# Converting the second weight matrix inside the last pair of the first stage

## The chip, the cores and the metric

The program runs on one core of a Trainium2 chip. Its time is the device time of one execution in microseconds, us. The kernel before took 2138.25 us, the median of three runs (2136.12 to 2142.62 us). The execution that the profiler recorded took 2138.95 us, and its span, first to last instruction, is 2137.1 us.

## The reference

The input x has 10000 rows of 1024 columns, and there are 5000 edges (src, dst). Two layers follow each other:

```python
# layer 1: a graph convolution on the normalised rows
h = einsum('nd,od->no', layernorm(x), W) + b
deg = (edges that start in a row) + 1
norm = deg[row]**-0.5 * deg[col]**-0.5     # row, col: src, dst and the self loops
x = x + segment_sum(norm[:, None] * h[col], row)
# layer 2: a feed-forward layer with low-rank experts
z = layernorm(x)
base_out   = einsum('bsi,oi->bso', z, base_W) + base_b
shared_out = (z @ shared_A.T) @ shared_B.T
gate = softmax(z @ router_W.T + router_b);  the two largest are kept, normalised
routed_out = sum over 6 experts of gate * ((z @ routed_A.T) @ routed_B.T)
x = x + base_out + shared_out + routed_out
```

All is float32. The kernel splits each operand of a product into a high part (the value rounded by a copy to the type fp32r) and a low part (value minus high part), and adds three products: high by high, high by low, low by high.

## The kernel before

The 10000 rows are padded to 79 tiles of 128 rows. There are two stages, and the second reads rows that the first has written to DRAM.

**First stage.** It computes the rows h and the rows r = x plus the self term, and stores both (`h_rows`, `r_rows`). Seven tiles go singly, then 36 pairs of tiles, each by seven block products in place of eight (a Strassen scheme). The products are called A11, S1, S2, A12, S3, A22, S4 in the order in which TensorE (PE) runs them; each has 12 matmuls of 512 columns. A11 of a pair is run ahead, within the pair before. The weights have seven quarters, B11, T1, T2, B21, T3, T4, B22, one for each product in that order, and lie in seven regions of the on-chip memory. `product_at(p, n)` is the count of the semaphore `done` at which product n of pair p is finished. The names A11 to S4 and B11 to B22 are the numbers 0 to 6, so B11 stands for the product A11, T1 for S1, T2 for S2, B21 for A12, T3 for S3.

For each pair the results are four half rows: C11 and C21 are written by ScalarE (ACT) in `weigh_part`, C22 and C12 by VectorE (DVE) in `finish_part`. `weigh_sum` on ACT copies a running sum out of a bank of the accumulator memory (PSUM) into u2 or u3. PE's product A22 waits for u3 (`u3_ok`), and S4 waits for C22 (`part_ok[C22]`). Each finished half row is stored by SyncE's queue (SP) in `store_part`. After all four, DVE computes two rows r (`residual`, L1406) and SP stores them.

**Between the stages.** The second weights are 8 blocks of 128 by 1142 values (`load_base`, L480), with 113 rows of small weights beside them (`bl_raw`). Each block is split by `base_high(k)` on ACT (L918) and `base_low(k)` on DVE (L1541), and the small weights likewise (L999, L1548). These blocks overwrite the regions of the first weights: block 0 to 2 as loaded lie in the region of B11, blocks 3 to 6 reach into that of T1, block 7 into T2, and the high parts lie in T2, B21 and, for blocks 6 and 7, T3. Hence the waits on `done`.

GpSimd (POOL) waits until the four half rows of the last pair have landed in DRAM (L694), passes a branch (L695) that is not taken when no row has too many edges, signals `rows_ready`, and then begins the gathers: it runs a one-column instruction that carries a wait (`carry_wait`, L552) and issues the indirect DMAs (L746, L728) which fetch rows of `h_rows` by edge. SP loads `r_rows` (L538) after `rows_ready` and after all rows r are stored.

**Second stage.** A software pipeline over 79 tiles: gathered rows are added to r on DVE, normalised on DVE, POOL and ACT, transposed and split, and multiplied with the 8 blocks on PE (L1032 to L1034, 72 matmuls a tile). Each engine goes through its instructions in the order in which they are written; there is no planner. The order is what the change touches.

Of the kernel before, what the change touches and what calls it, by code (L numbers as in the profile page):

```python
# [5 lines left out]
F32 = mybir.dt.float32  # L6
# [4 lines left out]
ALU = mybir.AluOpType  # L11
# [11 lines left out]
KB = D // P  # L23
# [29 lines left out]
PAIRS = (TILES - HEAD) // 2  # L53
A11, S1, S2, A12, S3, A22, S4 = range(7)
B11, T1, T2, B21, T3, T4, B22 = range(7)
# [81 lines left out]
def gnn_ffn(nc, x, src, dst, w_t, b, base_t, b_low, router_b, out, deg_dram, spill_dram):  # L137
# [4 lines left out]
    with ExitStack() as ctx:  # L142
# [140 lines left out]
        base_lo, o = place("base_lo", [P, KB, BCOLS], F32R)  # L283
        base_raw = sb("base_raw", [P, KB, BCOLS], F32, o)
        base_hi = sb("base_hi", [P, KB, BCOLS], F32R)
# [109 lines left out]
        def product_at(p, n):  # L395

            if n == A11:
                return max(7 * p - 1, 1)
            return 7 * p + 1 + n + (n > S3 and p + 1 < PAIRS)
# [11 lines left out]
        def _(sp):  # L411
# [56 lines left out]
            def store_part(p, v):  # L468
                t, h = PARTS[v]
                sp.wait_ge(part_ok[v], p + 1)  # L470
                sp.dma_start(h_dram[rows(first(p) + t), half(h)], hrow[t][:, half(h)]) \
                    .then_inc(part_stored[v], 16)
# [13 lines left out]
            for p in range(PAIRS):  # L486
                if p == 0:
                    store_rows(HEAD - 1)
                else:
                    store_part(p - 1, C12)  # L490
                    for t in range(2):
                        store_rest(p - 1, t)
                if p == PAIRS - 1:
                    for n, ks in ((B11, range(3)), (T1, range(3, 7)), (T2, range(7, KB))):
                        sp.wait_ge(done, product_at(p, n))
                        for k in ks:
                            load_base(k)
                store_part(p, C11)
                if p > 0 and first(p - 1) + 6 < TILES:
                    sp.wait_ge(r_stored, 16 * first(p))  # L500
                    load_x(first(p - 1) + 6)
                    load_x(first(p - 1) + 7)
                if RANK_AT <= p + 1 < RANK_AT + CHUNKS // RANKED and p >= RANK_AT:
                    sp.wait_ge(ranked, p + 1 - RANK_AT)
                    load_sources(p + 1 - RANK_AT)
                if p == RANK_AT - 1:
                    sp.wait_ge(t_lo_ok, 16)
                    load_sources(0)
                if p == TABLE_AT:
                    sp.wait_ge(slots_put, 16 * CHUNKS)  # L510
                    sp.dma_start(offs[:].rearrange("p t r -> p (t r)"),
                                 slot_dram[0:SLOTS, :].rearrange("(p s) a -> p (s a)", p=P)) \
                        .then_inc(slots_in, 16)
                store_part(p, C22)
                if p == PAIRS - 1:
                    sp.wait_ge(done, product_at(p, T3))
                    for a, z in ((0, KLOW - 1), (KLOW - 1, KLOW)):
                        sp.dma_start(bl_raw[a:z, :], b_low[a:z, :]).then_inc(bl_in, 16)
                store_part(p, C21)
# [235 lines left out]
        def _(act):  # L755
# [144 lines left out]
            def weigh_part(p, v, n):  # L900

                t, h = PARTS[v]
                act.wait_ge(done, product_at(p, n))
                if p == 0:
                    act.wait_ge(dis_ok, len(FACTORS))
                    act.wait_ge(r_ok, HEAD - 1 + (t == 0))
                    act.wait_ge(h_stored[t], 16 * ((HEAD - 1 - t) // 2 + 1))
                else:
                    act.wait_ge(part_stored[v], 16 * p)
                    act.wait_ge(pair_r_ok, 2 * (p - 1) + t + 1)  # L910
                nc.scalar.activation(hrow[t][:, half(h)], bp[p % 2][BANK[n]][:], ACT.Copy,
                                     scale=dis[:, first(p) + t:first(p) + t + 1]) \
                    .then_inc(part_ok[v], 1)

            def base_high(k):
                act.wait_ge(weights_in[k], 48)
                act.wait_ge(done, product_at(PAIRS - 1, T3))
                nc.scalar.activation(base_hi[:, k, :], base_raw[:, k, :], ACT.Copy) \  # L918
                    .then_inc(rest_hi_ok, 1)

# [48 lines left out]
            for p in range(PAIRS):  # L969
                last_high(p)  # L970
                weigh_sum(p, S2, 0, u2, C12, u2_ok)
                if p + 1 < PAIRS:
                    first_row(p + 1)
                weigh_part(p, C11, A12)
                if p + 1 < PAIRS:
                    first_row_right(p + 1)
                    normalise(first(p + 1) + 1)
                    if p > 0:
                        begin_third(p + 1)
                weigh_sum(p, S3, 1, u3, C22, u3_ok)  # L980
                if p + 2 < PAIRS:
                    begin_first(p + 2)
                if p + 1 < PAIRS:
                    begin_second(p + 1)
                    second_row(p + 1)
                    sums_high(p + 1)
                if p + 2 < PAIRS:
                    normalise(first(p + 2))
                if p == PAIRS - 1:
                    base_high(0)  # L990
                    base_high(1)
                weigh_part(p, C21, A22)
                if p + 1 < PAIRS:
                    others_high(p + 1)

            for k in range(2, KB):
                base_high(k)
            act.wait_ge(bl_in, 32)
            nc.scalar.activation(bl_hi[:], bl_raw[:], ACT.Copy).then_inc(rest_hi_ok, 1)  # L999
# [233 lines left out]
        def _(dve):  # L1233
# [167 lines left out]
            def residual(p, t, vs):  # L1401

                for v in vs:
# [2 lines left out]
                nc.vector.scalar_tensor_tensor(xn[n % 6][:], xn[n % 6][:], sqd[:, n:n + 1],  # L1406
                                               hrow[t][:], ALU.mult, ALU.add).then_inc(pair_r_ok, 1)

            def left_low(p, n, raw):
                dve.wait_ge(left_hi_ok, left_at(p, n))  # L1410
                nc.vector.tensor_tensor(left_lo[n][:].rearrange("p k n -> p (k n)"), raw,
                                        left_hi[n][:].bitcast(F32).rearrange("p k n -> p (k n)"),
                                        ALU.subtract).then_inc(left_lo_ok, 1)
# [84 lines left out]
            for p in range(PAIRS):  # L1498
                if p == 0:
                    finish_rows(HEAD - 1)  # L1500
                    quarter_low(T4, t4, 12)
                else:
                    finish_part(p - 1, C12, S4, u2, u2_ok)
                left_low(p, S4, s4[:])
                if p == SLOT_AT + 2:
                    dve.wait_ge(max_done, 1)
                    link(nc.vector.tensor_reduce(over_max[0:1, :], bt[0][0:1, 0:P], AX.X, ALU.max))
                    nc.vector.tensor_copy(spill_flag[:], over_max[0:1, :]).then_inc(tables_ok, 1)
                if p > 0:
                    residual(p - 1, 0, (C11, C12))  # L1510
                    residual(p - 1, 1, (C22, C21))
                if p + 1 < PAIRS:
                    statistics(first(p + 1) + 1)
                    left_low(p + 1, A11, a11[:])
                    scales(first(p + 1) + 1)
                if RANK_AT <= p < RANK_AT + CHUNKS // RANKED:
                    ranks(p - RANK_AT)
                if p == SLOT_AT:
                    slot_table()
                if p == TABLE_AT + 1:  # L1520
                    dve.wait_ge(slots_in, 16)
                    link(nc.vector.tensor_scalar(taken[:], offs[:, :, 0:SKIPPED], float(NPAD), None,
                                                 ALU.is_lt))
                finish_part(p, C22, S1, u3, u3_ok)
                if p + 1 < PAIRS:
                    sums(p + 1)
                    if p + 2 < PAIRS:
                        statistics(first(p + 2))
                    left_low(p + 1, A12, left_raw[A12][:])
                    if p + 2 < PAIRS:  # L1530
                        scales(first(p + 2))
                    left_low(p + 1, A22, bt[1][:])
                    dve.wait_ge(s3_ok, p + 2)
                    left_low(p + 1, S3, left_raw[S3][:])
# [1 line left out]
            residual(PAIRS - 1, 0, (C11, C12))  # L1536
            residual(PAIRS - 1, 1, (C22, C21))

            def base_low(k):
                dve.wait_ge(rest_hi_ok, k + 1)  # L1540
                nc.vector.tensor_tensor(base_lo[:, k, :], base_raw[:, k, :],  # L1541
                                        base_hi[:, k, :].bitcast(F32), ALU.subtract) \
                    .then_inc(rest_lo_ok, 1)

            for k in range(KB):
                base_low(k)
            dve.wait_ge(rest_hi_ok, KB + 1)
            nc.vector.tensor_tensor(bl_lo[:], bl_raw[:], bl_hi[:].bitcast(F32), ALU.subtract) \  # L1548
# [198 lines left out]
```

## Time and profile before

| what | value |
|---|---|
| median of three runs | 2138.25 us |
| the profiled execution | 2138.95 us, its span 2137.1 us |
| PE busy | 2049.0 us (96%) |
| DVE busy | 1601.0 us (75%) |
| POOL busy | 793.7 us (37%) |
| ACT busy | 703.7 us (33%) |
| mean clock granted to PE | 0.986 of full |
| DMA, mean over the span | 155 GB/s |

The page cuts the span into 40 slices of 53.4 us. Each engine's line gives its busy share in tenths for each slice, 9 meaning 90% or more. The line PEclk gives the clock granted to PE in tenths of full. A wait is listed as the instruction that was idle, the arrow, and what it was released by. Times "from the span's start" are used throughout.

### The profile page before, as it was taken

How to read it: one execution, taken by the hardware profiler on the slowest of the kernel's cores; microseconds unless marked ns; L12 is line 12 of the kernel's file. 1: busy time of each engine (PE TensorE's matmuls, PEld its weight loads, DVE VectorE, ACT ScalarE, POOL GpSimd, SP SyncE). 2: the span in 40 equal slices, each digit the busy share in tenths (PEclk: the TensorE clock that was granted, in tenths of full speed). 3: DMA queues.
4: the chain of work that ended last, by engine and by line, in shares of the span. 5: the costliest groups of instructions: out<-in, count | busy, mean ns of one | idle time of the engine just before them, and what ended most of it. 6: DMA issues, size and time to landing. Idle time of an engine off the chain costs nothing.

```text
span 2137.1 us, 34748 instructions
## 1 busy us (share of the span) xinstructions
PE 2049.0 (96%) x11145; PEld 1880.3 (88%) x11145; DVE 1601.0 (75%) x4089; ACT 703.7 (33%) x1236; POOL 793.7 (37%) x932
## 2 busy tenths in 40 slices
PE   7999999999999999739999999999999999999999
PEld 6777777777787777539999999999999999999999
DVE  6877878787776666657777777777777777777774
ACT  4455555555555555411111112111111112121111
POOL 1802333333325200164344444444444444444430
PEclk9999999999999999969999999999999999999999
DMA  6523434343434534566555656555555656555541
GB/s 249 199 104 144 165 134 174 132 173 134 169 125 153 146 134 162 215 170 167 147 164 146 166 158 162 156 153 159 150 164 149 166 152 162 153 156 159 151 128 40
DMA packets 126946, 330.63 MB, mean 155 GB/s; under 512 B 32944, under 2 KB 35840, under 8 KB 126806
## 3 DMA queue, kind: packets, MB, share of 16 engines
q1 hardware_dynamic: 77462, 226.31, 30.1%
q0 software_dynamic: 49344, 102.80, 21.0%
q8 instruction: 46, 0.75, 0.2%
q14 instruction: 94, 0.77, 0.1%
HBM read 266.46 MB, written 125.55 MB: 183 GB/s over the span
## 4 chain that ended last, share of the span: by engine, by line
PE 53%; issue 26%; DVE 9%; POOL 8%; ACT 2%; DMA 1%; DVEq 0%; POOLq 0%; ACTq 0%
PE bo L1032 13%; PE bo L1033 13%; PE bo L1034 13%; PE bt L1064 3%; POOL counted L638 2%; POOL counts L652 2%; PE bo L1223 2%; POOL xpw L580 2%; PE bo L1227 2%; PE bo L1225 2%; POOL slots L659 2%; DVE xn L1406 1%; PE bo L1042 1%; PE bo L1046 1%; PE bo L1044 1%
## 5 line engine op out<-in xcount | busy, mean ns | idle before, releaser
L1032 PE MATMUL bo<-base_hi,z_hi 128*128 128x380 f32 (+1 forms) x1896 | 652.7, 344 | 9.1 <-issue 9.1
L1033 PE MATMUL bo<-base_lo,z_hi 128*128 128x380 f32 (+1 forms) x1896 | 639.0, 337 | 0.0
L1034 PE MATMUL bo<-base_hi,z_lo 128*128 128x380 f32 (+1 forms) x1896 | 638.9, 337 | 0.0
L1053 PE MATMUL bo<-wr_hi,left_hi 128*128 128x512 f32 x1008 | 402.7, 399 | 6.3 <-ACT bo L880 3.8
L1057 PE MATMUL bo<-wr_hi,left_lo 128*128 128x512 f32 x1008 | 394.2, 391 | 0.0
L1055 PE MATMUL bo<-wr_lo,left_hi 128*128 128x512 f32 x1008 | 393.9, 391 | 0.0
L1032 PEld LDWEIGHTS bo<-base_hi,z_hi 128*128 128x128 f32 x1896 | 357.8, 189 | 9.5 <-issue 9.5
L1034 PEld LDWEIGHTS bo<-base_hi,z_lo 128*128 128x128 f32 x1896 | 358.7, 189 | 0.0
L1033 PEld LDWEIGHTS bo<-base_lo,z_hi 128*128 128x128 f32 x1896 | 358.5, 189 | 0.0
L746 POOL DMA_INDIRECT g<-h_rows,row_now x237 | 306.6, 1294 | 90.3 <-issue 90.1
L580 POOL TENSOR_TENSOR xpw<-xpin,neg_half 128x1 f32<-128x1 f32 x79 | 72.5, 918 | 551.8 <-DVE xpin L1248 551.8
L1053 PEld LDWEIGHTS bo<-wr_hi,left_hi 128*128 128x128 f32 x1008 | 189.9, 188 | 56.8 <-issue 20.4
L1004 ACT ACTIVATE ex<-lg 128x6 f32<-128x6 f32 x79 | 16.4, 208 | 659.5 <-DVE lg L1650 659.5
L1057 PEld LDWEIGHTS bo<-wr_hi,left_lo 128*128 128x128 f32 x1008 | 189.7, 188 | 40.3
L1055 PEld LDWEIGHTS bo<-wr_lo,left_hi 128*128 128x128 f32 x1008 | 190.1, 189 | 36.3
L735 POOL TENSOR_TENSOR pw<-pin,neg_half 128x1 f32<-128x1 f32 x79 | 47.1, 596 | 460.5 <-DVE pin L1617 460.5
L1604 DVE SCALAR_TENSOR_TENSOR acc<-g,taken,acc 128x1024 f32<-128x1024 f32 x158 | 202.9, 1284 | 19.9 <-DMA g<-h_rows,row_now 9.0
L1639 DVE SCALAR_TENSOR_TENSOR acc<-acc,dis,bo 128x262 f32<-128x262 f32 (+2 forms) x237 | 126.1, 569 | 108.1 <-PE bo L1227 103.0
L1020 ACT ACTIVATE z<-acc,shift,scale 128x1024 f32<-128x1024 f32 x79 | 98.4, 1245 | 287.2 <-DVE shift L1629 287.2
L764 ACT ACTIVATE un<-xn,xshift,xscale 128x1024 f32<-128x1024 f32 x79 | 98.3, 1244 | 262.9 <-issue 262.5
L728 POOL DMA_INDIRECT g<-h_rows,row_now x79 | 124.5, 1576 | 39.1 <-issue 39.1
L1244 DVE BATCH_NORM_STATS2 xst<-xn 128x6 f32<-128x512 f32 x158 | 109.1, 690 | 10.1 <-DMA xn<-x 7.3
(176 smaller groups left out, 2975.9 us busy)
## 6 DMA issues: line engine op xcount, KB each, us to landing
xn<-x SPq DMA_DIRECT2D x79, 512.0 KB, 4.3
r_rows<-xn SPq DMA_DIRECT2D x79, 512.0 KB, 2.7
acc<-r_rows SPq DMA_DIRECT2D x79, 512.0 KB, 4.3
out<-acc SPq DMA_DIRECT2D x79, 512.0 KB, 4.8
h_rows<-hrow SPq DMA_DIRECT2D x144, 256.0 KB, 2.5
g<-h_rows,row_now POOLq DMA_INDIRECT x316, 6.2
base_raw<-base_t SPq DMA_DIRECT2D x8, 571.0 KB, 8.4
wr_raw<-w_t SPq DMA_DIRECT2D x16, 256.0 KB, 6.7
```

Source lines behind the costliest of these rows:

```text
L580: nc.gpsimd.tensor_tensor(xpw[t % 2][:], xpin[t % 2][:], neg_half[:, 0:1], ALU.pow) \
L728: nc.gpsimd.indirect_dma_start(g[q][SKIPPED][:], None, h_dram, bass.IndirectOffsetOnAxis(ap=row_now[q][:, ROUNDS - 1:ROUNDS], axis=0), bou ...
L746: nc.gpsimd.indirect_dma_start(g[q][r][:], None, h_dram, bass.IndirectOffsetOnAxis(ap=row_now[q][:, r:r + 1], axis=0), bounds_check=(NPAD ...
L1032: nc.tensor.matmul(ps, hi[:, k, :], m_hi[:, k, n], start=(k == 0), stop=False)
L1033: nc.tensor.matmul(ps, hi[:, k, :], m_lo[:, k, n], start=False, stop=False)
L1034: return nc.tensor.matmul(ps, lo[:, k, :], m_hi[:, k, n], start=False, stop=(ends and k == KB - 1))
L1053: nc.tensor.matmul(ps, left_hi[n][:, k, :], wr_hi[n][:, k, :], start=False, stop=False, skip_group_check=True)
L1055: nc.tensor.matmul(ps, left_hi[n][:, k, :], wr_lo[n][:, k, :], start=False, stop=False, skip_group_check=True)
L1057: last = nc.tensor.matmul(ps, left_lo[n][:, k, :], wr_hi[n][:, k, :], start=False, stop=(k == 3), skip_group_check=True)
L1244: rows_c.link(dve, nc.vector.bn_stats(xst[q][:, h, :], xt[:, half(h)]))
L1604: accs.link(dve, nc.vector.scalar_tensor_tensor(a[:], g[q][r][:], taken[:, bass.ds(n, 1), r], a[:], ALU.mult, ALU.add))
L1639: nc.vector.scalar_tensor_tensor(av, av, dis[:, bass.ds(t, 1)], ps, ALU.mult, ALU.add).then_inc(out_ok, 1)
```

## The change

Three loads go out one pair earlier, and six of the eight conversions are moved into the last pair's time. SP loads blocks 0 to 2 within the last pair but one, after its half row C22, once the last pair's A11 is finished. ACT converts blocks 0 to 2 between C11 and u3 of the last pair, and blocks 3 to 5 after u3, where blocks 0 and 1 stood. The wait in front of blocks 0 to 5 is for A12 of the last pair, in place of S3. DVE takes the low parts of blocks 0 to 2 ahead of C22 and those of 3 to 5 ahead of C12. The rest stays behind the last pair. No conversion, load or product is added or dropped.

```diff
@@ SP, in the loop over pairs
                 if p == PAIRS - 1:
-                    for n, ks in ((B11, range(3)), (T1, range(3, 7)), (T2, range(7, KB))):
+                    for n, ks in ((T1, range(3, 7)), (T2, range(7, KB))):
                         sp.wait_ge(done, product_at(p, n))
                         for k in ks:
                             load_base(k)
...
                 store_part(p, C22)
+                if p == PAIRS - 2:
+                    sp.wait_ge(done, product_at(PAIRS - 1, B11))
+                    for k in range(3):
+                        load_base(k)
@@ ACT
             def base_high(k):
                 act.wait_ge(weights_in[k], 48)
-                act.wait_ge(done, product_at(PAIRS - 1, T3))
+                act.wait_ge(done, product_at(PAIRS - 1, B21 if k < 6 else T3))
...
                 weigh_part(p, C11, A12)
+                if p == PAIRS - 1:
+                    for k in range(3):
+                        base_high(k)
...
                 if p == PAIRS - 1:
-                    base_high(0)
-                    base_high(1)
+                    for k in range(3, 6):
+                        base_high(k)
                 weigh_part(p, C21, A22)
...
-            for k in range(2, KB):
+            for k in range(6, KB):
                 base_high(k)
@@ DVE
+                if p == PAIRS - 1:
+                    for k in range(3):
+                        base_low(k)
                 finish_part(p, C22, S1, u3, u3_ok)
+                if p == PAIRS - 1:
+                    for k in range(3, 6):
+                        base_low(k)
...
-            for k in range(KB):
+            for k in range(6, KB):
                 base_low(k)
```

The function `base_low` itself only moves up in the text.

## Rows read from the trace of the kernel before

**Rows 1.** The page's slices: PE's busy share in tenths.
```profile
PE   7999999999999999739999999999999999999999
```
**Rows 2.** Windows: start:end and length, then busy us of PE, PEld, DVE, ACT, POOL, clock, DMA.
```profile
1605.00:2100.00 495.00, 494.25 (x2970) 491.98 (x2969) 378.68 (x1086) 92.00 (x198) 210.04 (x250) 1.00 0.55 149
```
**Rows 3.** The chain of waits between the stages: start, us, what held it.
```profile
895.39 0.76 DVE hrow L1397
896.17 6.93 DMA h_rows<-hrow
...
904.11 0.52 issue
...
910.15 1.11 POOL g L746
```
**Rows 4.** Timeline of POOL: start, us, instruction, [idle before, releaser].
```profile
903.55 6.43 POOL L552 TENSOR_TENSOR tick_pool<-neg_half 128x1 f32<-128x1 f32 x1 [34.52 <-DMA h_rows<-hrow]
955.72 1.08 POOL L552 TENSOR_TENSOR tick_pool<-neg_half 128x1 f32<-128x1 f32 x1 [0.76 <-DMA g<-h_rows,row_now]
```
**Rows 5.** Line L552 on POOL: count, duration in ns min/median/max.
```profile
L552 POOL TENSOR_TENSOR tick_pool<-neg_half x199: 182/193/6433, 172.2 to 2063.7; 128x1 f32<-128x1 f32 x199
```
**Rows 6.** Timeline of DVE, end of the first stage and one later place.
```profile
898.65 10.15 DVE L1541 TENSOR_TENSOR base_lo<-base_raw,base_hi 128x1142 fp32r<-128x1142 f32 x8
908.71 1.22 DVE L1548 TENSOR_TENSOR bl_lo<-bl_raw,bl_hi 113x1024 fp32r<-113x1024 f32 x1
916.37 2.60 DVE L1604 SCALAR_TENSOR_TENSOR acc<-g,taken,acc 128x1024 f32<-128x1024 f32 x2 [6.44 <-DMA g<-h_rows,row_now]
955.53 1.22 DVE L1612 TENSOR_TENSOR acc<-acc,g 128x1024 f32<-128x1024 f32 x1
```
**Rows 7.** Timeline of ACT in the last pair.
```profile
886.12 0.69 ACT L911 ACTIVATE hrow<-bo,dis 128x512 f32<-128x512 f32 x1 [2.03 <-PE bo L1057]
888.83 0.69 ACT L897 ACTIVATE u<-bo,dis 128x512 f32<-128x512 f32 x1 [2.03 <-PE bo L1057]
889.42 2.19 ACT L918 ACTIVATE base_hi<-base_raw 128x1142 fp32r<-128x1142 f32 x2
899.87 1.16 ACT L918 ACTIVATE base_hi<-base_raw 128x1142 fp32r<-128x1142 f32 x1 [0.67 <-DMA base_raw<-base_t]
```
**Rows 8.** Timeline of PE: an earlier gap, last A22, start of second stage, later gap.
```profile
732.26 1.06 PE L1064 MATMUL bt<-ident,un 128*128 128x128 f32 x8 [3.15 <-DVE left_lo L1411]
889.67 0.47 PE L1053 MATMUL bo<-wr_hi,left_hi 128*128 128x512 f32 x1 [0.87 <-ACT u L897]
928.18 1.97 PE L1064 MATMUL bt<-ident,z 128*128 128x128 f32 x8 [32.83 <-ACT z L1020]
954.90 0.34 PE L1217 MATMUL bt<-ident,hs 128*113 128x128 f32 x1 [2.65 <-DVE z_lo L1683]
```
**Rows 9.** Timeline of SP's queue: a half-row store of pair 34, the base loads.
```profile
872.60 0.33 SPq L471 DMA_DIRECT2D h_rows<-hrow  x1
882.56 5.24 SPq L480 DMA_DIRECT2D base_raw<-base_t  x8
```
**Rows 10.** Line L471 (half-row stores), from 840 to 910 us.
```profile
DMA to landing us min/median/max: 2.0/2.5/12.3
```
**Rows 11.** Line L480 (base loads).
```profile
DMA to landing us min/median/max: 5.6/8.4/12.8
```
**Rows 12.** Line L538 (loads of r_rows), from 860 to 930 us.
```profile
DMA to landing us min/median/max: 3.3/7.5/13.8
```
**Rows 13.** Windows of 2 us, columns as in rows 2.
```profile
874.00:876.00 2.00, 2.00 (x11) 1.65 (x10) 1.97 (x4) 1.91 (x5) 0.00 (x0) 1.00 0.06 23
898.00:900.00 2.00, 0.00 (x0) 0.00 (x0) 2.00 (x3) 1.28 (x2) 0.00 (x0) 0.50 1.06 375
904.00:906.00 2.00, 0.00 (x0) 0.00 (x0) 2.00 (x2) 0.00 (x0) 2.00 (x1) 0.50 0.04 16
956.00:958.00 2.00, 2.00 (x8) 1.80 (x6) 1.93 (x3) 1.05 (x2) 1.84 (x2) 0.50 0.08 23
```

More of the change, by code:

```diff
@@ L1407, in residual, with base_low @@
                                                hrow[t][:], ALU.mult, ALU.add).then_inc(pair_r_ok, 1)
+            def base_low(k):
+                dve.wait_ge(rest_hi_ok, k + 1)
+                nc.vector.tensor_tensor(base_lo[:, k, :], base_raw[:, k, :],
+                                        base_hi[:, k, :].bitcast(F32), ALU.subtract) \
+                    .then_inc(rest_lo_ok, 1)
             def left_low(p, n, raw):
@@ L1537, in _ @@
             residual(PAIRS - 1, 1, (C22, C21))
[L1539 to L1543, printed above, removed]
-            for k in range(KB):
+            for k in range(6, KB):
                 base_low(k)
```

## The prediction

> **What bounds the kernel now.** I read the page's slices first. PE is full in all but three slices of 53.4 us: the first, and the two from 855 to 962 us, where it falls to 7 and 3 tenths [rows 1]. PE's own rows give the reason: one wait of 32.83 us, until 928.18, for the first normalised tile of the second stage [rows 8]. After that start PE is busy 494.25 of 495 us [rows 2], so the second stage lasts as long as its matmuls, wherever it begins. A microsecond gained or lost ahead of that start is a microsecond of the end. The change touches nothing outside this place, and the question is what the 32.8 us consist of.
>
> The chain of waits gives it in order [rows 3]. DVE, which waits for the last product, writes the last half row C12 from 895.39 on (0.76 us); its store lands after 6.93 us; POOL starts its waiting instruction L552 at 903.55; and the first gather goes out at 910.15. The reader is to see that the piece between the two is the interesting one: L552 is recorded with 6.43 us [rows 4], while its median over 199 is 193 ns [rows 5]. It ended at 909.98. DVE's eight low parts and the small one run without a break from 898.65 to 909.93 [rows 6]. The same coincidence stands elsewhere: the L552 of 955.72 lasts 1.08 us and ends at 956.80, and DVE's L1612 ends at 956.75 [rows 4, 6]. I read this as POOL being held while DVE runs operations on two operands of the on-chip memory. If so, the conversions are on the path, through POOL and not through PE, which needs the blocks only some 30 us later.
>
> **The change part by part, against the profiled execution (2138.95 us).**
>
> Loads. Blocks 0 to 2 go out behind the store of pair 34's C22 at 872.60, so from about 873 us; three issues at 5.24/8 = 0.66 us each end near 875, before that pair's next store is due (its ACT result comes at about 876). The DMA engines are nearly free there (share 0.06 at 874 to 876 [rows 13]). SP waits for A11 of the last pair, which is through by then, so nothing queues behind this wait. Cost nothing. In the last pair five loads stand where eight stood, from 882.56 on [rows 9]. At 375 GB/s [rows 13] a block of 0.585 MB takes 1.56 us, so 4.7 us of transfer leave the saturated time.
>
> Store of C12. It was issued at about 896.2 and took 6.93 us [rows 3], where half-row stores have a median of 2.5 us [rows 10]. The extra 4.4 us I read as the backlog of base loads, the last of which lands only at 899.87 [rows 7]. With 4.7 us less traffic the backlog is gone before C12. Bounds: 2.0 us (shortest row) to 6.93 us (unchanged). I take 3, near the median because that row is of the same transfer with free engines.
>
> ACT ahead of u3. C11 starts at 886.12 and the next ACT instruction can start 0.59 us later, as block 0 does after u3 (888.83 to 889.42 [rows 7]). Three conversions at a pitch of 1.04 (2.19 for two, less the last one's 1.15) to 1.16 (one alone) take 3.1 to 3.5 us, so u3 starts at 889.8 to 890.2 instead of 888.83. PE's A22 starts 0.84 us after u3 [rows 7, 8]: at 890.7 to 891.0 instead of 889.67. Nothing hides this; PE ends its last product 1.0 to 1.4 us later, and I take 1.2. This is the price of the change.
>
> ACT and DVE after it. Blocks 3 to 5 occupy ACT from 890.6 to 894.0; A22 ends at about 893.6 (from 889.67 to C12 at 895.39 PE ran two products, 24 matmuls, 2.75 us a product at 0.23 each with 0.2 until DVE starts), so C21 is late by 0.3 us, and it isn't the last half row. Block 5 must have landed by 892.8: it is the third of its batch, first landing 5.6 us after 882.56 [rows 11] plus two blocks, 891.3 us. On DVE the low parts run at a pitch of 1.26 us ((908.71 - 898.65)/8 [rows 6]). Blocks 0 to 2 end at about 891.7, when block 2 comes from ACT at 890.05; C22 (0.76 like C12) follows until 892.5, and S4 isn't due on PE before 893.6. Cover 1.1 us. Blocks 3 to 5 end at about 896.2, and S4 ends at 896.4. Cover only 0.2 us; if block 5 is later than thought, C12 and all behind it slip by the same amount.
>
> DVE at the end. Before, from the start of C12 (895.39) to the end of the small low part (909.93) it was 14.54 us without a pause. Six low parts leave: 6 x 1.26 = 7.55, and 6.99 remain. C12 starts at 896.6, so DVE is done at 903.6. C12 lands at 897.4 + 3 = 900.4, and POOL arrives at 900.8, within DVE's run, as before. It is freed at 903.6 instead of 909.98, and the first gather goes out at 903.85 instead of 910.15: 6.3 us earlier.
>
> From there everything shifts with it, with one new meeting. The loads of r_rows start once the last rows r are stored. They were issued behind DVE's residuals, which shift by 1.2 us only, so the load of the first r tile (1.4 us of transfer) meets the first gathers, where there was a free stretch before (share 0.04 at 904 to 906 [rows 13]). Bounds 0 to 1.4 us; I take 0.2, since the gathers' data follow their issue by some 2 us.
>
> Sum: +1.2 (u3) - 7.55 (six low parts) + 0.05 (rounding) + 0.2 = -6.1 us. The profiled execution would take 2132.85 us. It lies 0.7 us above the median of the runs shown, so by the median 2138.25 - 6.1 = 2132.2 us.
>
> A rule of the Trainium skill speaks to the held instruction. "SBUF — State Buffer", in the part on engine and DMA ports, says that a VectorE operation with two SBUF inputs and a GpSimd instruction that reads SBUF exclude each other for one whole instruction, the loser blocking. The rows show the exclusion, but over more than one instruction: the L552 of 903.55 let four ends of DVE instructions go by and came through only at the end of the run. If the lock were given up at each instruction, POOL would have passed near 904.8 already. I go by the rows; the other reading is the first rival.
>
> **The rivals.**
>
> POOL gets in early. If the hold is released at the first end of a DVE instruction, or if DVE has a pause in front of block 6, POOL passes right at 900.8 and the gather goes out at 901.5 (0.19 for L552, 0.52 issue [rows 3, 5]). Gain 8.6 us, 2129.6 us. Against it are the ends passed over at 905 to 908.7. Chance 0.12.
>
> The store is not shortened. C12 lands after 6.93 us again, at 904.3, and DVE is done by then. The gather goes out at 904.8 + 0.71 = 905.5. Gain 4.6 us, 2133.6 us. For it speaks that the small loads and the store of C21 still stand ahead of it; against it, the median of 2.5. Chance 0.10.
>
> DVE isn't what holds POOL. If the 6.6 us between POOL's arrival and the first gather are a fixed cost of this start (a branch stands in front of it), only the store's backlog is won: 900.8 + 6.6 = 907.4, gain 2.8 us, 2135.5 us. Against it are the two ends that agree within 0.05 us. Chance 0.10.
>
> The clock falls in the gap ahead of A22. The gap grows from 0.87 to about 2.1 us. A gap of 3.15 us at 729 to 732 left the clock at full; one of 2.65 us before 954.90 was followed by half clock from 956 on [rows 8, 13]. If it falls, the 24 matmuls of A22 and S4 cost up to 24 x 0.23 = 5.4 us more, nearly the whole gain: about 2137.6 us. Chance 0.06.
>
> Slower than before: the load of the first r tile queues behind the gathers. DVE's first instruction of the second stage needs it and the first gathered rows; before, it started at 916.37 on the gathers' landing [rows 6]. Loads of this line take from 3.3 to 13.8 us [rows 12]. By the forecast DVE starts there 6.1 us earlier, at 910.3. A load issued at about 903.2 has 7.1 us until then, and each further microsecond goes off the gain; from 13.2 us on the gain is gone, and at 13.8 us it lands at 917.0, 0.6 us later than before: 2138.9 us. For it: the load and the gathers start together now. Against it: the load's issue is still ahead of the gathers'. Chance 0.04.
>
> **How the numbers follow.** Forecast 0.58, rivals 0.12, 0.10, 0.10, 0.06, 0.04. About 0.3% (6.4 us) is what a measurement can tell from no change; faster means below 2131.8 us. The forecast lies almost on this line: half of it counts as faster (0.29), with the first rival 0.41. Slower by 0.3% needs two mishaps: 0.03. The range takes the forecast's own 2130.5 to 2134, the first two rivals and the third: 2129 to 2136.5 us.
>
> **What would show it.** L552 between the stages should take some 3 us and end with DVE's small low part, near 903.6. The store of C12 should take about 3 us, the gap ahead of A22 about 2 us at full clock, and the three early loads should stand at 873 us. DVE's run behind C12 should hold two low parts. The first gather should stand near 904, PE's long wait should be 25.5 us (32.8, begun 1.2 later, ended 6.1 earlier). The prediction is wrong if L552 keeps its 6.4 us with DVE idle, if u3 or C12 start later than 890.3 or 897.2, or if the time from first gather to first transposes (18.0 us) changes by more than 1 us.

## The result, and the profile after

The changed kernel takes 2130.24 us, the median of 6 runs (2126.13 to 2132.16), against 2137.8 us for the kernel before on the same chip (6 runs). The ratio is 0.9967, 95% interval 0.9956 to 0.9977. Timed once more on another chip, with 7 runs, it gave 2131.22 against 2136.89 us, ratio 0.9970 (0.9959 to 0.9982). The forecast was 2132.2 us, 6.1 us below the kernel before; measured were 7.6 and 5.7 us. The profiled execution has a span of 2130.3 us (before: 2137.1).

The three early loads stand where the prediction put them, as SP's timeline of the changed kernel shows; this answers to [rows 9]:

```profile
873.64 1.40 SPq L480 DMA_DIRECT2D base_raw<-base_t  x3
```

Then the chain of waits of the changed kernel between the stages, which answers to [rows 3]. L552 is L556 here, and L746 is L750.

```profile
898.70 0.76 DVE hrow L1404
...
899.48 2.02 DMA h_rows<-hrow
...
901.94 0.56 POOL tick_pool L556
...
903.51 2.03 POOL g L750
```

The store of C12 takes 2.02 us instead of 6.93, POOL's waiting instruction is followed by the first gather at 903.51 instead of 910.15, but C12 itself begins 3.3 us later than in [rows 3] (0.7 us of it because the whole last pair stands later in this execution). POOL's own timeline of the changed kernel, which answers to [rows 4]:

```profile
901.94 1.41 POOL L556 TENSOR_TENSOR tick_pool<-neg_half 128x1 f32<-128x1 f32 x1 [32.24 <-DMA h_rows<-hrow]
903.51 2.03 POOL L750 DMA_INDIRECT g<-h_rows,row_now  x1 [0.16 <-issue]
```

And DVE's, which answers to [rows 6]:

```profile
888.56 3.87 DVE L1418 TENSOR_TENSOR base_lo<-base_raw,base_hi 128x1142 fp32r<-128x1142 f32 x3 [5.74 <-ACT base_hi L922]
...
893.01 3.85 DVE L1418 TENSOR_TENSOR base_lo<-base_raw,base_hi 128x1142 fp32r<-128x1142 f32 x3
898.70 0.75 DVE L1404 SCALAR_TENSOR_TENSOR hrow<-bo,dis,u 128x512 f32<-128x512 f32 x1 [1.84 <-PE bo L1064]
...
901.95 2.60 DVE L1418 TENSOR_TENSOR base_lo<-base_raw,base_hi 128x1142 fp32r<-128x1142 f32 x2
904.47 1.22 DVE L1561 TENSOR_TENSOR bl_lo<-bl_raw,bl_hi 113x1024 fp32r<-113x1024 f32 x1
912.58 2.60 DVE L1617 SCALAR_TENSOR_TENSOR acc<-g,taken,acc 128x1024 f32<-128x1024 f32 x2 [6.89 <-DMA g<-h_rows,row_now]
```

The low parts of blocks 0 to 5 stand ahead of C12, and the run behind it is two low parts and the small one. From the start of C12 to the end of the run it is 905.69 - 898.70 = 6.99 us, as forecast. But POOL's L556 (901.94, 1.41 us) ended at 903.35, with the end of the first of these low parts, 2.3 us ahead of the run's end. ACT's timeline of the changed kernel in the last pair answers to [rows 7]:

```profile
886.79 0.69 ACT L915 ACTIVATE hrow<-bo,dis 128x512 f32<-128x512 f32 x1 [2.03 <-PE bo L1064]
887.38 3.23 ACT L922 ACTIVATE base_hi<-base_raw 128x1142 fp32r<-128x1142 f32 x3
890.52 0.68 ACT L901 ACTIVATE u<-bo,dis 128x512 f32<-128x512 f32 x1
891.09 3.24 ACT L922 ACTIVATE base_hi<-base_raw 128x1142 fp32r<-128x1142 f32 x3
```

PE's rows for the last A22 and for the start of the second stage answer to [rows 8]:

```profile
891.34 0.47 PE L1060 MATMUL bo<-wr_hi,left_hi 128*128 128x512 f32 x1 [1.86 <-ACT u L901]
...
922.31 1.97 PE L1071 MATMUL bt<-ident,z 128*128 128x128 f32 x8 [23.65 <-ACT z L1027]
```

Then the changed kernel's windows around that gap, columns as in [rows 2]; the last three numbers are the granted clock, the DMA share and GB/s:

```profile
890.00:892.00 2.00, 0.66 (x3) 0.61 (x4) 2.00 (x2) 2.00 (x3) 0.00 (x0) 1.00 1.01 388
892.00:894.00 2.00, 2.00 (x7) 1.54 (x6) 2.00 (x3) 2.00 (x3) 0.00 (x0) 0.59 0.94 360
894.00:896.00 2.00, 2.00 (x7) 1.57 (x6) 2.00 (x3) 0.39 (x2) 0.00 (x0) 0.56 0.91 281
896.00:898.00 2.00, 2.00 (x10) 1.66 (x9) 0.86 (x1) 2.00 (x3) 0.00 (x0) 1.00 0.48 189
```

The gap ahead of A22 is 1.86 us, and behind it the clock is down to half (1.2 GHz) for most of the time from 892.3 to 895.7: matmuls stand 0.43 us apart instead of 0.23.

Executions of one kernel differ by some microseconds in how long the first stage takes (the last pair's u2 starts between 881.9 and 887.9 us in the profiles below, and at 883.39 and 884.96 in the two of the kernel before). So I measure all places from the start of u2; of what the edits move, only the three early loads stand ahead of it:

| kernel | u3 | C12 | POOL arrives | first gather | first transposes | first products |
|---|---|---|---|---|---|---|
| before | 5.44 | 12.00 | 20.16 | 26.76 | 44.79 | 55.89 |
| before, again | 5.44 | 12.00 | 20.85 | 26.75 | 44.46 | 55.57 |
| changed | 6.45 | 14.63 | 17.87 | 19.44 | 38.24 | 49.06 |
| changed, again | 6.45 | 14.61 | 17.85 | 19.42 | 38.94 | 50.15 |
| changed, third | 6.45 | 14.64 | 17.87 | 19.45 | 38.35 | 49.11 |
| loads only (e1) | 5.44 | 12.00 | 15.25 | 16.82 | 38.44 | 49.43 |
| conversions only (e7) | 8.63 | 17.66 | 21.62 | 22.47 | 42.04 | 53.24 |
| before, low parts late (e2) | 5.44 | 12.00 | 19.62 | 20.38 | 44.39 | 52.70 |
| the same, second profile (e8) | 5.44 | 12.00 | 20.86 | 21.62 | 45.41 | 53.65 |
| conversions in idle (e3) | 5.44 | 12.00 | 15.41 | 16.81 | 36.32 | 47.18 |
| the same, tail late (e4) | 5.44 | 12.00 | 16.83 | 17.59 | 37.79 | 49.62 |
| e3 with the first low part early (e11) | 5.44 | 12.00 | 16.35 | 17.11 | 36.24 | 39.67 |
| loads only, POOL later (e9) | 5.44 | 12.00 | 19.26 | 26.75 | 44.79 | 56.27 |
| loads only, POOL later, with a memset (e10) | 5.44 | 12.00 | 19.29 | 26.75 | 44.69 | 56.10 |

"POOL arrives" is the start of its first waiting instruction, L552 (or L556). Each entry is a start read from the kernel's timelines, less the start of u2 there (before: 883.39; changed: 884.07). After the first products PE runs to the end in 1194.3 to 1197.8 us in all but e11.

### The profile page after: what moved, and what is told of

It reads as the page before. It is cut to its first block, busy times and chain, and to the rows that moved or that the text cites. A ratio compares the mean times of both kernels' runs of the same rounds, so it can differ in the third digit from the quotient of the medians.

```text
span 2130.3 us, 34748 instructions
## 1 busy us (share of the span) xinstructions
PE 2051.9 (96%) x11145; PEld 1883.3 (88%) x11145; DVE 1600.5 (75%) x4089; ACT 703.4 (33%) x1236; POOL 788.0 (37%) x932
## 4 chain that ended last, share of the span: by engine, by line
PE 55%; issue 25%; POOL 8%; DVE 8%; ACT 2%; DMA 1%; DVEq 0%; POOLq 0%; ACTq 0%
PE bo L1039 14%; PE bo L1040 14%; PE bo L1041 14%; PE bt L1071 4%; POOL counted L642 2%; POOL counts L656 2%; PE bo L1230 2%; PE bo L1234 2%; POOL xpw L584 2%; PE bo L1232 2%; POOL slots L663 2%; PE bo L1049 1%; PE bo L1051 1%; PE bo L1053 1%; DVE xn L1413 1%
## 5 line engine op out<-in xcount | busy, mean ns | idle before, releaser
L750 POOL DMA_INDIRECT g<-h_rows,row_now x237 | 308.3, 1301 | 90.7 <-issue 90.7
```

What stands on the lines that cost most here:

```text
L750: nc.gpsimd.indirect_dma_start(g[q][r][:], None, h_dram, bass.IndirectOffsetOnAxis(ap=row_now[q][:, r:r + 1], axis=0), bounds_check=(NPAD ...
```

## The experiments

The theories: A, POOL is held until DVE's whole run of low parts ends, as forecast; B, POOL passes at the next end of a DVE instruction; C, the time between POOL's arrival and the first gather is fixed. And beside them the question which half of the change carries the gain.

**The loads alone (e1).**
```diff
@@ the kernel before, SP
-                    for n, ks in ((B11, range(3)), (T1, range(3, 7)), (T2, range(7, KB))):
+                    for n, ks in ((T1, range(3, 7)), (T2, range(7, KB))):
...
+                if p == PAIRS - 2:
+                    sp.wait_ge(done, product_at(PAIRS - 1, B11))
+                    for k in range(3):
+                        load_base(k)
```


> The kernel before with the change's loads alone: blocks 0 to 2 behind the last but one pair's C22, all conversions where they were. Both theories: the store of C12, issued at about 896.2, lands in 2 to 3 us instead of 6.93, and POOL arrives at L552 at about 899.2 instead of 903.55. Theory A (POOL is held until DVE's run of low parts ends): L552 then lasts 10.7 us, the first gather stays at 910.15, the time is the one of before (0.0 us). Theory B (POOL passes at the end of one DVE instruction): L552 ends at a boundary of the low parts, 900 to 901.3, the first gather goes out at about 901.5, and the time falls by 4 to 8 us. Theory C (a fixed 6.6 us from POOL's arrival to the first gather): gather at 905.8, time down by 4.3 us.

Measured: 2131.75 against 2137.81 us, ratio 0.9970 (0.9957 to 0.9983). The loads alone give as much as the whole change, within what the times can tell. Only the loads were moved, and the store of C12 took 2.02 us, so the backlog is confirmed as its cause. The timeline of POOL in this kernel:

```profile
903.14 1.40 POOL L556 TENSOR_TENSOR tick_pool<-neg_half 128x1 f32<-128x1 f32 x1 [29.61 <-DMA h_rows<-hrow]
904.71 2.03 POOL L750 DMA_INDIRECT g<-h_rows,row_now  x1 [0.16 <-issue]
907.04 2.12 POOL L750 DMA_INDIRECT g<-h_rows,row_now  x1 [0.30 <-issue]
909.46 2.19 POOL L750 DMA_INDIRECT g<-h_rows,row_now  x1 [0.30 <-issue]
911.68 0.41 POOL L556 TENSOR_TENSOR tick_pool<-neg_half 128x1 f32<-128x1 f32 x1
```

And of DVE:

```profile
903.14 10.15 DVE L1545 TENSOR_TENSOR base_lo<-base_raw,base_hi 128x1142 fp32r<-128x1142 f32 x8
...
914.35 2.60 DVE L1608 SCALAR_TENSOR_TENSOR acc<-g,taken,acc 128x1024 f32<-128x1024 f32 x2
```

POOL arrived as the run began and passed at the end of the first low part (1.40 us); then its gathers were issued 2.34 and 2.42 us apart, against 1.42 and 1.32 in the kernel before, where DVE was idle by then. Theory A fails here, and C as well. But DVE's first addition follows its run without a pause (914.35), and so the first transposes are 6.4 us earlier, not 9.9 like the first gather: with the gathers early, DVE's run is on the path by itself.

**The low parts held back until the first gather has landed, in the kernel before (e2, timed as e8).**
```diff
+            dve.wait_ge(g_in[0][SKIPPED], 16)
             for k in range(KB):
                 base_low(k)
```


> The kernel before, with DVE's eight low parts and the small one held back until the first gather has landed, so that DVE is idle when POOL arrives. Theories A and B: L552 takes its usual 0.19 us, and the first gather goes out at 904.3 instead of 910.15. Theory C (fixed cost): L552 still takes 6.4 us and the gather stays at 910.15. The whole time should not fall much, since the 11.3 us of low parts now start at about 908.6 and end at 920, later than the 916.37 at which DVE's first addition started: +3 us to the start of the second stage, more if POOL's next gathers are held by the run.

> The kernel before with DVE's low parts held back until the first gather has landed, timed. Its single execution took 2132.64 us, its first gather stood 20.4 us behind the start of u2 against 26.8 in the kernel before. If DVE's run in front of POOL's first gathers is what costs the kernel before: 3 to 6 us faster than before. If that execution was a draw: within 1.5 us of before.

Measured: e2 2132.64 us in one run, e8 2134.08 against 2138.14 us, ratio 0.9979 (0.9969 to 0.9988). With the store as slow as before (6.39 and 7.64 us) L552 took 0.19 us and the gather followed 0.76 us behind it, as POOL's timeline of e2 shows:

```profile
902.49 0.19 POOL L552 TENSOR_TENSOR tick_pool<-neg_half 128x1 f32<-128x1 f32 x1 [33.96 <-DMA h_rows<-hrow]
903.25 1.11 POOL L746 DMA_INDIRECT g<-h_rows,row_now  x1 [0.57 <-issue]
```

So DVE's run is what holds L552 in the kernel before; a fixed cost (C) is excluded. The first transposes came neither earlier nor the 3 us later that I had expected (44.39 and 45.41, against 44.79 and 44.46); of the gain of 4 us, 1.9 to 3.2 us stand at the next step, the first products, and where the rest comes from isn't shown. There DVE waited less for the second tile's gathers, which had landed meanwhile (in e2 its two waits were 0.82 and 1.85 us, in the kernel before 2.33 and 2.52). I had expected hardly any gain from e2 and was wrong on that; for e8 the 4.1 us lie in the range written for it.

**The kernel before and the changed one, profiled again (e5, e6, e12; no edit).**

> The kernel before, unchanged, profiled a second time. In the first profile POOL's L552 was held for 6.43 us, past four ends of DVE instructions, while in the loads-only kernel the same instruction met the same run of low parts and lasted 1.40 us. If POOL is always held to the end of DVE's run in this kernel: L552 lasts until the end of the small low part again, about 6.4 us. If what a POOL instruction waits for is normally one DVE instruction and the first profile was an unlucky draw: L552 lasts 0.2 to 2.6 us and the first three gathers are issued 2.3 to 2.5 us apart, ahead of the end of the run. The store of C12 takes 6 to 7 us in both.

> The changed kernel, unchanged, profiled a second time. The order of work says: gap ahead of A22 1.9 us, store of C12 about 2.0 us, L552 1.2 to 1.4 us, first gather at 19.4 us behind the start of u2 (in the first profile 884.07 to 903.51). The clock of the last pair may differ: if it falls after every gap of 1.9 us, A22 and S4 take 7.3 us again; if it is a draw, they take 5.7 us in some executions.

> The changed kernel, unchanged, timed beside the others on one chip. About 2130.5 us; the kernel with the conversions in ACT's idle stretches should stand 1.5 to 2.6 us below it. Its profile should show the gap of 1.86 us ahead of A22 with half clock behind it a third time, if such a gap always costs the clock at this place.

Measured for the kernel before (2139.54 us), first POOL's timeline:

```profile
905.81 5.73 POOL L552 TENSOR_TENSOR tick_pool<-neg_half 128x1 f32<-128x1 f32 x1 [35.22 <-DMA h_rows<-hrow]
```

Then DVE's last row of the run:

```profile
910.27 1.22 DVE L1548 TENSOR_TENSOR bl_lo<-bl_raw,bl_hi 113x1024 fp32r<-113x1024 f32 x1
```

L552 ended at 911.54 and the run at 911.49 (910.27 + 1.22). The long hold is no draw. The changed kernel repeats as well: L556 took 1.41, 1.41 and 1.42 us. The gap of 1.86 us was followed by half clock in all three profiles (C12 at 14.63, 14.61, 14.64), but that is no proof that it always is. PE has two gaps earlier in the first stage which no edit touches, and there one kernel goes either way. [rows 8] has 3.15 us of gap ahead of 732.26 in the kernel before, at full clock. In its second profile, e5, PE's timeline has this in the same place:

```profile
733.19 1.94 PE L1064 MATMUL bt<-ident,un 128*128 128x128 f32 x8 [3.42 <-DVE left_lo L1411]
```

And the window behind that gap:

```profile
733.00:735.00 2.00, 1.81 (x9) 1.84 (x10) 2.00 (x5) 0.96 (x3) 0.00 (x0) 0.50 0.23 83
```

The clock is at half (1.2 GHz), and eight transposes take 1.94 us in place of 1.06. Over all fourteen profiles the clock fell at this gap (2.20 to 3.94 us long) in five, and at another, near 643 us (2.25 to 2.29 us long), in seven. The two earlier gaps are a draw, then, and three of three ahead of A22 can't rule out a draw there. The 0.87 us of the other kernels was followed by full clock in ten profiles of ten.

The times were 2131.85 and, timed, 2131.22 us.

**POOL's arrival moved inside the run (e9, e10), in the loads-only kernel.**
```diff
                     pool.wait_ge(row_copied, t + 1)
+                    if isinstance(t, int) and t == 0:
+                        pool.wait_ge(rest_lo_ok, 3)
+                        nc.gpsimd.memset(tick_pool[:, 13:14], 0.0)     # e10 only
                     carry_wait(5 + 4 * (s.q % 2))
```


> The loads-only kernel, with POOL's L552 held back until DVE has ended the third of its eight low parts, so that it is issued within 0.1 us of an instruction's end, in the middle of the run and not at its start. If the long hold of the kernel before (6.43 and 5.73 us) comes from arriving in the middle of the run: L552 lasts 7 to 8 us, until the small low part ends. If POOL passes at the next end whenever it is in line at the start of a DVE instruction: 1.2 to 1.4 us.

> As the kernel in which POOL waits for the third low part's end, with a one-column memset (it only writes) ahead of L552, so that L552 arrives 0.2 to 0.6 us into the fourth low part. If the phase inside a DVE instruction decides: a long hold here (5 us or more) and a short one without the memset. If the place in the run decides: both alike. If neither: 0.7 to 1.1 us here, the rest of the fourth low part.

The timeline of POOL in e9:

```profile
901.55 7.33 POOL L556 TENSOR_TENSOR tick_pool<-neg_half 128x1 f32<-128x1 f32 x1 [33.64 <-DVE base_lo L1547]
```

Of DVE in e9:

```profile
897.54 10.15 DVE L1547 TENSOR_TENSOR base_lo<-base_raw,base_hi 128x1142 fp32r<-128x1142 f32 x8
907.61 1.22 DVE L1554 TENSOR_TENSOR bl_lo<-bl_raw,bl_hi 113x1024 fp32r<-113x1024 f32 x1
```

Of POOL in e10:

```profile
903.54 0.10 POOL L749 MEMSET tick_pool<- 128x1 f32 x1 [33.61 <-DVE base_lo L1548]
903.60 7.30 POOL L556 TENSOR_TENSOR tick_pool<-neg_half 128x1 f32<-128x1 f32 x1
```

Both were held to the run's end: 7.33 us, to 908.88, with the run's end at 908.83, and 7.30 us. The loads-only kernel with POOL arriving at the third low part's end has the first gather of the kernel before (26.75). So its late arrival alone takes away what the early loads had won; the times, 2135.28 and 2136.62 us, one run each, lie among those of the kernel before (2134.57 to 2138.79, median 2136.89). The stage's first L552 passed at the next end when it arrived before or within the run's first low part (e1, changed three times, e3, e7, e11), and was held to the end when it came later (before twice, e9, e10).

The phase within an instruction doesn't explain it. The two edits came out 0.03 us apart (0.23 and 0.26 us into the fourth low part), so the memset tests it hardly at all; but the kernel before arrived 1.13 us into a low part, e5 0.57 us, and both were held to the end too.

The place in the run is not the whole rule either. L552 runs again for the next gathers, and in the kernels with a long run some of these later ones fall in its middle. In e1 one begins at 911.68, in the seventh low part, and takes 0.41 us. In e2, first POOL's timeline:

```profile
913.10 1.20 POOL L552 TENSOR_TENSOR tick_pool<-neg_half 128x1 f32<-128x1 f32 x1
```

Then DVE's run in e2:

```profile
907.87 10.16 DVE L1541 TENSOR_TENSOR base_lo<-base_raw,base_hi 128x1142 fp32r<-128x1142 f32 x8 [9.66 <-DMA g<-h_rows,row_now]
```

At 1.26 us each, 913.10 lies in the fifth low part, which ends at 914.25. L552 ended at 914.30, with four instructions of the run still to come; e8 repeats it (1.20 us). These passed at the next end although they came in the middle of the run, 0.19 us into a low part. What sets them apart from the four that were held is that POOL had been at work since the run's first low part. A memset ahead of L552, which only writes, doesn't make the difference (0.10 us in e10, and L552 was held all the same). What does stays open.

**The conversions alone (e7).** The changed kernel with all eight loads where they were before: the edit is the reverse of e1's on SP.

> The changed kernel with all eight loads where they stood before: the conversions' new order alone. ACT stands at block 0 ahead of u3 until it lands, some 5.6 us after the first issue at 882.56, and at block 2 until about 891.4, so u3 starts near 892.5 instead of 888.8 and the gap ahead of A22 is 4.5 us, with the half clock after it. The backlog stays, less the 3.7 us by which C12 is late. If the early loads carry the gain (they shorten the store, and the conversions' order is only a cost): 1 to 4 us slower than before. If the six conversions taken out of DVE's run carry it: 2 to 4 us faster than before.

Measured: 2134.01 against 2138.14 us, ratio 0.9981 (0.9971 to 0.9990), 4.1 us faster, where 2 to 4 were expected. u3 is 3.2 us later (3.7 expected), PE's gap ahead of A22 is 4.05 us with half clock behind it, and C12 is 5.7 us later; yet the first gather is 4.3 us earlier. A late C12 meets no backlog (store 2.73 us), and POOL arrives in the run's first low part and passes after 0.69 us. So the conversions' order gains by the hold (0.69 us in place of 6.43), and pays for the store's gain with C12's lateness; the early loads gain by store and hold (2.02 and 1.40 us). The two halves overlap (4.1 and 6.1 us apart, 7.6 and 5.7 together), since both take POOL's first L552 out of the middle of DVE's run.

**The conversions where ACT is idle (e3).**
```diff
@@ the changed kernel, ACT
-                act.wait_ge(done, product_at(PAIRS - 1, B21 if k < 6 else T3))
+                act.wait_ge(done, product_at(PAIRS - 1, T2 if k < 2 else B21 if k < 6 else T3))
...
+                if p == PAIRS - 1:
+                    base_high(0)
+                    base_high(1)
                 weigh_part(p, C11, A12)
                 if p == PAIRS - 1:
-                    for k in range(3):
-                        base_high(k)
+                    base_high(2)
```


> The changed kernel with ACT's conversions of blocks 0 and 1 moved ahead of C11 (waiting for S2 of the last pair in place of A12), block 2 behind C11, and 3 to 5 behind u3 as they were, so that u3 is not delayed. If the delayed u3 and the half clock after it cost the changed kernel 1.0 and 1.6 us: the gap ahead of A22 is 0.9 us, no window in the last pair is below full clock, C12 starts 2.6 us earlier, and the time falls by 2 to 2.6 us against the changed kernel (about 2127.6). If these microseconds were hidden behind POOL's wait: no change within 1 us.

Measured: 2128.90 us (2128.05 to 2130.05) against 2137.81, ratio 0.9954 (0.9942 to 0.9967). ACT had 2.03 us idle ahead of C11 and 2.03 ahead of u3 [rows 7]; the three conversions fit there, as ACT's timeline of e3 shows:

```profile
886.17 2.20 ACT L922 ACTIVATE base_hi<-base_raw 128x1142 fp32r<-128x1142 f32 x2
888.31 0.69 ACT L915 ACTIVATE hrow<-bo,dis 128x512 f32<-128x512 f32 x1
888.89 1.15 ACT L922 ACTIVATE base_hi<-base_raw 128x1142 fp32r<-128x1142 f32 x1
891.03 0.69 ACT L901 ACTIVATE u<-bo,dis 128x512 f32<-128x512 f32 x1 [0.98 <-PE bo L1066]
```

And PE's row for the last A22:

```profile
891.86 0.47 PE L1062 MATMUL bo<-wr_hi,left_hi 128*128 128x512 f32 x1 [0.87 <-ACT u L901]
```

u3 is at 5.44 again, the gap at 0.87 us, the clock full, and C12 at 12.00: the 2.6 us are back. The first transposes come 1.9 to 2.6 us earlier than in the three profiles of the changed kernel. In time the ratios differ by 0.0013 and 0.0016, 2.8 to 3.4 us, with intervals that overlap, so the times alone don't show that it beats the changed kernel. They do show it for the loads alone, timed beside it on one chip (2130.66 to 2134.14 us, against 2128.05 to 2130.05).

**The same with DVE's tail behind the gather (e4).**
```diff
+            dve.wait_ge(g_in[0][SKIPPED], 16)
             for k in range(6, KB):
                 base_low(k)
```


> As the kernel with the conversions in ACT's idle stretches, and DVE's two last low parts and the small one held back until the first gather has landed. Theory A (POOL held to the end of DVE's run): the first gather goes out near 900.7 instead of about 903, and the second stage starts 0.5 us or more earlier, bounded by the 3.7 us of low parts that now sit between the first gathers' landing and the first addition. Theory B (POOL passes at the next end of an instruction): the gather moves by less than 1 us, and the second stage starts about 1.3 us later, since DVE is busy with low parts when the gathered rows land.

Measured: 2129.04 against 2137.81 us, ratio 0.9957 (0.9946 to 0.9969): the same as e3. L556 took 0.19 us, but its store took 3.61 us, so the first gather came 0.8 us later by the mark, not earlier, and the first transposes 1.5 us later, as theory B has it.

**e3 with the low parts of the second stage's first tile taken early (e11).**
```diff
-                if s.has(1):
+                if s.has(1) and s.has(0):
                     low_parts(s)
...
+                    if isinstance(s.i, int) and s.i == -2:
+                        low_parts(Step(-1, DEEP - 1))
                     acc_statistics(s)
```


> The kernel with the conversions in ACT's idle stretches, and in addition the low parts of the second stage's first tile taken on DVE ahead of the statistics of the second tile, where DVE waits some 2.4 us for a gather. PE's first products of the second stage then start near 927 instead of 932.8 and are over when the second tile is ready to be transposed. If PE's start is bound by its own order: 1.5 to 2.5 us faster than without this (about 2126.8). If the second tile's gathers bind it all the same: no change within 0.5 us.

Measured: 2127.54 against 2136.89 us, ratio 0.9959 (0.9945 to 0.9972). PE's first products start 7.5 us earlier by the mark, but PE then waits 4.14 us for z_lo of a later step, and all but 0.6 us is given back by the end (u2 to the end of the span 1242.0 us against 1242.6). The time can't be told from that of e3; the 1.5 to 2.5 us that were expected did not come.

## Why the prediction was right, and where not

The time came out within the range and 2 us from the forecast, but by luck in part: two of the prediction's own signs of being wrong came true. C12 started at 898.70, later than 897.2 even when the 0.7 us by which u2 stood later are taken off, and in one profile of three the time from first gather to first transposes changed by more than 1 us. The steps, in the order in which the prediction has them:

- A microsecond ahead of the second stage is one of the end. Right: from the first products to the end PE needs 1194.3 to 1197.8 us with no relation to the edits, apart from e11.
- The loads cost nothing and go where the DMA engines are free. Right: they were issued from 873.64 on, and with the loads alone (e1) u3 and C12 stand at 5.44 and 12.00, as before.
- Store of C12: 3 us taken, 2.02 us in three profiles (2.01 in one of them). Its cause, the backlog, is shown by e1. In e4 and e11, with the same early loads, it took 3.61 and 3.13 us.
- u3 1.2 us late. Measured 6.45 - 5.44 = 1.01 us; e3 removes it.
- The clock in the gap ahead of A22: given 0.06, and it fell in all three profiles. The rival was mis-sized too: not 5.4 but 2.63 - 1.01 = 1.6 us, since the clock came back after some eight matmuls. That a gap of 3.15 us in [rows 8] had left the clock full was a poor guide: it was one draw, and in the second profile of the same kernel (e5) the clock fell there.
- DVE's run ends 6.99 us behind the start of C12: exact. Blocks 3 to 5 did not delay C12, whose own lateness covered them.
- POOL is held to the end of DVE's run. This step failed for the changed kernel, while it is right for the kernel before (e2, e5). The forecast had "it is freed at 903.6" with the run's end; by the measured run the end would have been 905.69, and POOL passed at 903.35. The first rival (0.12) is what happened: POOL arrived with the run's first low part and passed at its end. Neither the prediction's rule nor the other one alone is right. The prediction also counts the ends wrongly that L552 let go by in the kernel before. They were five, the first of them at 903.76, so that one is where it would have passed, and not 904.8. The Trainium skill's page "SBUF — State Buffer" (section "SBUF: two separate sides") has the port pair held for one instruction: the changed kernel agrees (1.41 us), e9 does not (7.33 us, past five ends of DVE instructions).
- The meeting of loads and gathers: 0.2 us taken. From first gather to first transposes it is 18.8, 19.5 and 18.9 us against 18.03: 0.8 to 1.5 us.

So the terms were wrong with opposite signs: C12 was 1.4 us later than forecast and the way from first gather to first transposes took 0.6 to 1.3 us more than the 0.2 allowed, while POOL passed 2.3 us before the run's end. The sum came out by their cancelling, at 6.5, 5.9 and 6.4 us for the first transposes, where 6.1 was forecast. And the price I set on six low parts, 7.55 us, is not theirs alone: e1 has all eight in the run and is as fast.

## What to carry to other kernels

At a hand-over between stages, ask at which point of another engine's run of work an instruction arrives, not only how long the run is: here an arrival 4.0 us later (e9 against e1) turned a hold of 1.4 us into one of 7.3. One profile can show as settled what is a draw, as with the clock behind a gap; look at the same gap in a second one. Clear the DMA queues ahead of the one store that the next stage waits for. Work that is moved into a busy stretch goes into an engine's idle gaps of its own length; three conversions ahead of u3 cost 2.6 us on the matmul chain (1.0 by the wait, 1.6 by the half clock behind it), while the same three in two gaps of 2 us cost nothing.

## What the runs showed of the hardware

The first POOL instruction of the stage that reads the on-chip memory, while DVE ran two-operand instructions back to back, was held for 5.73 to 7.33 us when it arrived after the first of a run (four profiles), and 0.30 to 1.42 us when it arrived before or within the first (seven profiles). Later ones of the same kind that arrived in the middle of a run passed at the next end (0.41 us in e1, 1.20 us in e2 and e8). What makes the difference stays open. POOL's indirect DMAs were slowed but not held to the end: in e1 they went out 2.3 to 2.4 us apart within the run.

After the gap of 1.86 us in the last pair TensorE's clock fell to half in three profiles of three, after one of 4.05 us (e7) in the only one, and with a gap of 0.87 us in none of ten. Of two gaps earlier in the first stage, one of 2.25 to 2.29 us was followed by half clock in seven profiles of fourteen, one of 2.20 to 3.94 us in five of fourteen. Length alone doesn't decide there: 3.55 us left it full in e3, 2.34 us did not in the changed kernel.
